# A graph network kernel: the order of weighing and digit reading, and of aggregating and turning the counts

## The chip, the cores and the metric

The kernel runs on one core of one Trainium2 chip. Its time is the device time of one execution in microseconds (us), given as the median of several runs.

## The reference

The input is a graph of 1250 nodes with 128 features each, and 20000 edges (src, dst) with four edge attributes. Two layers run one after the other, each with a residual.

```python
# layer 1: attention over the incoming edges, then one GRU step
h = relu(layernorm(x))
Wh = h @ W.T + b_W
e = leaky_relu((Wh @ a_src)[src] + (Wh @ a_dst)[dst] + a_b, 0.2)
attn = segment_softmax(e, dst)                # over the edges of one dst
h_prime = segment_sum(attn * Wh[src], dst) + h @ res_W.T + res_b
x = x + gru(h_prime, h)
# layer 2: four steps; an edge's type is the argmax of its attributes
h = relu(layernorm(x))
for _ in range(4):
    trans = einsum('nd,tod->tno', h, W_edge) + b_edge
    h = gru(segment_sum(trans[type, src], dst), h)
x = x + h
```

## The kernel before, in words

The nodes are padded to NT = 10 tiles of 128. The kernel never gathers edges in layer 1. It builds, for each block of 128 destination nodes (J or n, 0 to 9), a matrix of how many edges of each type run from each source to each destination, packed as digits, and computes attention densely on it.

A block has two windows of 64 destinations, numbered 2J and 2J+1. The edges are sorted by destination, and a window takes the edge tiles in which its destinations lie: 8 to 10 from J = 3 on (constant `TILES`). Per tile VectorE makes a one-hot row set (`one_hots`, line 967) in a ring of `RING = 12` slots, and TensorE multiplies it with a one-hot of the source lane and sums in PSUM (`window`, line 1468). VectorE may be at most 12 ahead (line 965). In some windows `one_hots` first makes a slice of lane one-hots (line 941, constant `LANES_MADE`; from J = 3 on for windows 7, 10 and 14).

The work on a block then passes over the engines:

- `evac(J, half)`, ScalarE, line 544: copies a window's sums from PSUM to SBUF. It waits for the window, and, as the target is used again, for `read_digits(J - 1)`.
- `read_digits(n)`, VectorE, lines 975 and 976: splits the words of block n into digits. It waits for both evacuations of the block.
- `count_turn(n)`, TensorE, line 1482: turns the digits into rows of counts in PSUM. It waits for the digits, and until the counts before have been copied out.
- `counts_out(n)` and `excesses(n)`, ScalarE, lines 556 and 562: copies the counts to SBUF and checks digits that ran over. It waits for `count_turn(n)` and for `weigh(n - 1)`, which reads the same buffer.
- `weigh(n)`, VectorE, line 986: ten instructions that multiply the counts with the attention weights. It waits for `counts_out(n)` (semaphore `K.counted`) and for `aggregate(n - 2)`.
- `aggregate(n)`, TensorE, line 1505: twenty matmuls with the weighed counts, whose last column is the denominator. It waits for `weigh(n)`.
- `reciprocals(n)`, VectorE, lines 1015 and 1019, waits for `aggregate(n)`; `attn_out(n)`, ScalarE, line 584, scales the result.

Each engine runs its list in the order written. On all three engines that order is by hand, in a function `turn(J)`. ScalarE's `turn(J)` (line 610) is: `evac(J - 1, 1)`, `attn_out(J - 3)`, `evac(J, 0)`, `counts_out(J - 1)`, `excesses(J - 1)`. VectorE's is at line 1021 and TensorE's at line 1520.

Behind the ten turns stands a tail. ScalarE has `evac(9, 1)`; VectorE has `read_digits(9)`, `weigh(8)`, `reciprocals(8)`, `weigh(9)`; TensorE has the residual matmuls, the first gates, `count_turn(9)`, `aggregate(8)`, and later `aggregate(9)` (lines 1666 to 1677). Then come layer 1's GRU and the four steps of layer 2, which don't use `turn`.

Of the kernel before, what the change touches and what calls it, by code (L numbers as in the profile page):

```python
# [93 lines left out]
def build(nc, x, src, dst, attr, W, b_W, a_src, a_dst, a_b, res_W, res_b, Wi, Wh_g, bi, bh,  # L94
          W_edge, b_edge, W_ih, W_hh, b_ih, b_hh, out):
    with ExitStack() as ctx:
# [212 lines left out]
        def there(n):  # L309
            return not isinstance(n, int) or 0 <= n < NT  # L310

        def later(n, k=1):
            return not isinstance(n, int) or n >= k


        def tile_ranges(eng, J):
            word = eng.value_load(table[0:1, J:J + 1], min_val=0, max_val=(1 << 26) - 1)
            first = eng.snap(word & 255)
            starts = [first]
            for shift in (8, 14, 20):  # L320
                starts.append(eng.snap(first + ((word >> shift) & AHEAD)))
            return (starts[0:2], starts[2:4])
# [42 lines left out]
        def weights(n):  # L365
            return exp_b if isinstance(n, int) and n % 2 else exp_a
# [484 lines left out]
        def _(dve):  # L851
# [58 lines left out]
            def edge_scales():  # L910
                dve.wait_ge(E1.bound, 1)
                up, down = edge_up[:].bitcast(I32), edge_down[:, 0:1].bitcast(I32)
                link(v.tensor_scalar(edge_up[:], edge_q[:, 3:4], ROOM, None, ALU.mult))
                link(v.tensor_scalar(up, up, 23, 23, ALU.logical_shift_right, ALU.logical_shift_left))
                v.tensor_scalar(down, up, -1.0, float(263 << 23), ALU.mult, ALU.add).then_inc(E1.scale, 1)
# [42 lines left out]
            def one_hots(j, starts):  # L958
                for k in range(LANES_MADE[j - 1] if j else 0, LANES_MADE[j]):
                    lane_hots(k)  # L960
                dve.wait_ge(K.cellw, j + 1)
                for b, before, tiles in window_hots(j, starts):
                    end = before + len(tiles)
                    if end > RING:
                        dve.wait_ge(K.slot, end - RING)
                    for q, tile in enumerate(tiles):
                        last = v.tensor_scalar(half_hot[:, (before + q) % RING], iota[:, b * HALF:(b + 1) * HALF],  # L967
                                               cell_w[:, j % CELL_SETS, bass.ds(tile, 1)],
                                               fields[:, 1, bass.ds(tile, 1)], ALU.is_equal, ALU.mult)
                    last.then_inc(K.pair, len(tiles))  # L970

            def read_digits(n):
                dve.wait_ge(K.evac, 2 * n + 2)
                pk = packed.rearrange("p (i d) -> p i d", i=NT)
                v.tensor_scalar(nibbles[:, 0, :, n * P:(n + 1) * P], pk, LOW_NIBBLES, None, ALU.bitwise_and)
                v.tensor_scalar(nibbles[:, 1, :, n * P:(n + 1) * P], pk, 4, LOW_NIBBLES,  # L976
                                ALU.logical_shift_right, ALU.bitwise_and).then_inc(K.digits, 1)

            def weigh(n):
                dve.wait_ge(K.counted, n + 1)  # L980
                if n == 0:
                    dve.wait_ge(S0.fallen, 1)
                if n >= 2:
                    dve.wait_ge(K.agg, n - 1)
                for i in range(NT):
                    last = v.scalar_tensor_tensor(weights(n)[:, i * P:(i + 1) * P], fall[:, n * P:(n + 1) * P],  # L986
                                                  s_tall[:, i:i + 1], count[:, i * P:(i + 1) * P], ALU.max, ALU.mult)
                last.then_inc(K.probs, 1)
# [24 lines left out]
            def reciprocals(n):  # L1013
                dve.wait_ge(K.agg, n + 1)
                v.tensor_scalar(denom[:], psD[:, P:P + 1], 1e-30, None, ALU.max).then_inc(K.denom, 1)
                dve.wait_ge(K.denom, n + 1)
                if later(n):
                    dve.wait_ge(K.attn, n)
                v.reciprocal(denom_r[:], denom[:]).then_inc(K.recip, 1)

            def turn(J):
                if there(J):
                    one_hots(2 * J, ranges[J][0])
                if J == 3:
                    reciprocals(0)
                if there(J - 1):
                    read_digits(J - 1)
                if J == 1:
                    peaks()
                    edge_scales()  # L1030
                if there(J - 2):
                    weigh(J - 2)
                if there(J):
                    one_hots(2 * J + 1, ranges[J][1])
                if there(J + 1):
                    ranges[J + 1] = tile_ranges(dve, J + 1)
                if J >= 3:
                    reciprocals(J - 2)

            def peaks():  # L1040
                dve.wait_ge(S0.s_rows, 1)
                v.tensor_reduce(s_peak[:], s_rows[:], AX.X, ALU.max).then_inc(S0.s_peak, 1)
                dve.wait_ge(S0.s_peak, 1)
                v.tensor_scalar(s_back[:], s_peak[:], dst_bias[:, 0:1], RISE, ALU.add, ALU.mult)
                link(v.tensor_scalar(s_up[:], s_src[:], s_peak[:, 0:1], SLOPE, ALU.subtract, ALU.mult))
                link(v.tensor_reduce(s_top[:], s_up[:], AX.X, ALU.min))
                v.tensor_scalar(s_up[:], s_up[:], -SLOPE * SPREAD, None, ALU.max).then_inc(S0.s_fall, 1)
# [3 lines left out]
            for J in range(NT):  # L1051
                turn(J)
# [328 lines left out]
        def _(pe):  # L1381
# [21 lines left out]
            def spans():  # L1403
                for lo in range(0, NP, 512):
                    yield lo, min(NP, lo + 512)
# [44 lines left out]
            def fall_rows():  # L1450
                pe.wait_ge(S0.s_rows, 1)
                for lo, hi in spans():
                    last = mm(smallf[:, lo:hi], b_cols[:], hT[:, lo:hi], start=True, stop=True)
                last.then_inc(S0.d_ps, 1)


            def window(j, half, starts, begin=0, until=NW * ETP):
                if later(j, 2):
                    pe.wait_ge(K.evac, j - 1)
                pe.wait_ge(S0.lanes, LANES_MADE[j])  # L1460
                for b, before, tiles in window_hots(j, starts):
                    if not begin <= before < until:
                        continue
                    end = before + len(tiles)
                    pe.wait_ge(K.pair, end)
                    for q, tile in enumerate(tiles):
                        u = before + q - HOTS_BEFORE[2 * j + b]
                        last = mm(big[:, 2 * half + b, 0:HALF],  # L1468
                                  lane_hot[:, :, bass.ds(tile, 1)].rearrange("p l a -> p (l a)"),
                                  half_hot[:, (before + q) % RING], start=(u == 0),  # L1470
                                  stop=(u == TILES[2 * j + b] - 1), skip_group_check=True)
                    last.then_inc(K.slot, len(tiles))
# [22 lines left out]
            def aggregate(n):  # L1495
                fast = isinstance(n, int)
                if fast:
                    pe.wait_ge(K.probs, n + 1)
                else:
                    pe.wait_ge(K.probsb, n + 1)  # L1500
                if later(n):
                    pe.wait_ge(K.attn, n)
                w = weights(n) if fast else probT
                for i in range(NT):
                    last = mm(psD[:, 0:P + 1], w[:, i * P:(i + 1) * P], Wh[:, i], start=(i == 0),  # L1505
                              stop=(i == NT - 1), skip_group_check=True)
                last.then_inc(K.agg, 1)
# [12 lines left out]
            def turn(J):  # L1520
                lower, upper = tile_ranges(pe, J)
                window(2 * J, 0, lower)
                if J == 1:
                    fall_rows()
                if J >= 2:
                    count_turn(J - 1)
                if J == 2:
                    edge_weights()
                if J >= 3:
                    aggregate(J - 2)  # L1530
                window(2 * J + 1, 1, upper)
                if J == 1:
                    count_turn(0)
# [12 lines left out]
            score_rows()  # L1546
            pe.wait_ge(C.ident16, 1)
            turn(1)
            turn(2)
            edge_biases()  # L1550
            pe.wait_ge(E1.rows, 1)
# [371 lines left out]
```

## Time and profile before

| | |
|---|---|
| median of 3 runs | 425.48 us (425.25 to 427.06) |
| profiled execution | 426.4 us, of it span 424.4 us |
| TensorE matmul busy | 367.2 us (87%) |
| VectorE busy | 265.5 us (63%) |
| ScalarE busy | 150.5 us (35%) |
| GpSimd busy | 100.6 us (24%) |
| mean granted TensorE clock | 0.974 |

The span is the time from the first to the last instruction of the profiled execution. Busy shares are means over stages with different limits. The attention stage with its turns lies between 23 and 158 us; from 178 us on the four steps of layer 2 run, in which TensorE is busy 232.34 of 246 us. The granted clock is TensorE's, as a share of the full 2.4 GHz; 0.50 is the level of 1.2 GHz.

### The profile page before, as it was taken

What the parts mean: (1) busy time and instruction counts of PE and PEld (TensorE: products, weight loads), DVE (VectorE), ACT (ScalarE), POOL (GpSimd) and SP (SyncE); (2) the same over time, 40 slices, a digit from 0 to 9 for tenths busy, and PEclk for the clock granted to TensorE, in tenths of its full rate; (3) what the DMA queues carried; (4) which work ended last, traced back from release to release, by engine and by line L of the source; (5) the groups of instructions that cost most, each with busy time, mean ns of one, the idle gap of its engine ahead of it and who ended that gap; (6) DMA issues with size and microseconds to landing.
All of it is one profiled execution on the core that took longest, in us unless ns stands there. A gap on an engine that the chain in (4) does not pass through costs nothing.

```text
span 424.4 us, 6625 instructions
## 1 busy us (share of the span) xinstructions
PE 367.2 (87%) x2057; PEld 247.0 (58%) x2057; DVE 265.5 (63%) x797; ACT 150.5 (35%) x333; POOL 100.6 (24%) x139
## 2 busy tenths in 40 slices
PE   1479758878798978888999999999999999999993
PEld 0457434656555866533557574756746575747792
DVE  6899958899989548686274544444443545434144
ACT  3354565444454535533122231322322232213021
POOL 3101100000000001010477400777003774007300
PEclk9999987999989989999999999999999999999997
DMA  5200000000000000112224201133202242012200
GB/s 146 73 1 2 0 2 1 2 1 2 2 1 2 0 2 0 49 51 102 73 53 151 81 34 74 45 105 100 87 2 93 58 148 87 26 74 52 56 14 23
DMA packets 14498, 19.88 MB, mean 47 GB/s; under 512 B 2591, under 2 KB 7728, under 8 KB 14460
## 3 DMA queue, kind: packets, MB, share of 16 engines
q1 hardware_dynamic: 10276, 12.90, 8.6%
q0 software_dynamic: 2912, 5.97, 5.7%
q10 hardware_dynamic: 1272, 0.54, 0.5%
q8 instruction: 19, 0.31, 0.3%
q14 instruction: 19, 0.16, 0.1%
HBM read 8.27 MB, written 11.13 MB: 46 GB/s over the span
## 4 chain that ended last, share of the span: by engine, by line
PE 69%; DVE 18%; issue 5%; ACT 4%; DVEq 2%; POOL 1%; DMA 0%; SPq 0%; ACTq 0%; POOLq 0%
PE small L1626 28%; PE big L1608 7%; PE small L1505 6%; PE big L1468 6%; DVE scores L986 3%; DVE cell_hot L967 3%; PE small L1482 3%; PE small L1647 2%; PE small L1660 2%; PE big L1571 1%; DVEq L967 1%; PE small L1571 1%; PE small L1562 1%; PE small L1573 1%; DVE digit_words L1137 1%
## 5 line engine op out<-in xcount | busy, mean ns | idle before, releaser
L1626 PE MATMUL small<-nibbles,store 128*128 128x384 fp8e4 (+1 forms) x640 | 125.8, 353 | 1.6 <-DVE store L1141 0.8
L482 POOL DMA_INDIRECT scores<-messages,w_gat x91 | 87.9, 966 | 120.5 <-DMA messages<-store 94.0
L1626 PEld LDWEIGHTS small<-nibbles,store 128*128 128x128 f16 x640 | 62.3, 98 | 64.6 <-issue 7.5
L967 DVE TENSOR_SCALAR cell_hot<-iota,cell_w,fields 128x320 bf16<-128x320 f16 x231 | 64.9, 358 | 0.9 <-issue 0.3
L1468 PE MATMUL big<-cell_hot,store 128*128 128x320 bf16 x231 | 44.8, 331 | 15.2 <-DVE cell_hot L967 12.9
L740 ACT CAST store<-digit_words 128x512 f16<-128x512 f32 x40 | 24.6, 618 | 81.6 <-DVE digit_words L1137 81.6
L1137 DVE TENSOR_TENSOR digit_words<-big,edge_rows 128x512 f32<-128x512 f32 x40 | 27.4, 690 | 40.0 <-PE big L1608 40.0
L1468 PEld LDWEIGHTS big<-cell_hot,store 128*128 x231 | 31.6, 145 | 26.1 <-issue 23.3
L1608 PE MATMUL big<-wT,h 128*128 128x512 f32 x80 | 38.6, 599 | 2.3 <-ACT h L736 2.3
L468 POOL TENSOR_TENSOR rstd<-var_e,power 128x2 f32<-128x2 f32 x5 | 3.5, 694 | 135.8 <-DVE var_e L1125 135.8
L1080 DVE SCALAR_TENSOR_TENSOR cell_hot<-rz,cell_hot 128x256 f32<-128x256 f32 (+2 forms) x29 | 11.0, 380 | 36.1 <-ACT cell_hot L711 36.1
L1482 PE MATMUL small<-nibbles,ident 128*128 128x512 fp8e4 (+1 forms) x120 | 26.4, 375 | 6.7 <-DVE nibbles L976 6.7
L1141 DVE TENSOR_TENSOR store<-digit_words,store 128x512 f16<-128x512 f32 x40 | 27.5, 689 | 6.1 <-ACT store L740 4.8
L710 ACT ACTIVATE rz<-small,gb 128x192 f32<-128x192 f32 (+1 forms) x14 | 6.2, 444 | 67.9 <-PE small L1573 67.9
L1505 PE MATMUL small<-Wh,scores 128*128 128x129 f32 x200 | 26.4, 290 | 2.7 <-DVE scores L986 1.7
L1505 PEld LDWEIGHTS small<-Wh,scores 128*128 128x128 f32 x200 | 24.8, 202 | 5.5 <-DVE scores L986 3.6
L986 DVE SCALAR_TENSOR_TENSOR scores<-scores,s_tall,tallies 128x128 f32<-128x128 f32 x100 | 27.1, 345 | 0.3 <-issue 0.3
L1482 PEld LDWEIGHTS small<-nibbles,ident 128*128 128x128 f16 x120 | 12.0, 105 | 20.8 <-DVE nibbles L976 8.6
L1253 DVE TENSOR_SCALAR aS<-small,edge_down 128x192 f32<-128x192 f32 (+2 forms) x24 | 9.7, 431 | 22.5 <-PE small L1626 17.6
L1608 PEld LDWEIGHTS big<-wT,h 128*128 128x128 f32 x80 | 14.5, 190 | 15.4 <-issue 10.6
L544 ACT CAST digit_words<-big 128x640 uint16<-128x640 f32 x20 | 13.8, 692 | 22.1 <-DVE nibbles L976 12.6
L556 ACT ACTIVATE tallies<-small 128x1280 f32<-128x1280 f32 x10 | 12.4, 1240 | 19.7 <-DVE scores L986 10.6
(262 smaller groups left out, 489.5 us busy)
## 6 DMA issues: line engine op xcount, KB each, us to landing
messages<-store SPq DMA_DIRECT2D x40, 256.0 KB, 2.0
scores<-messages,w_gat POOLq DMA_INDIRECT x91, 2.6
xn<-in_x SPq DMA_DIRECT2D x1, 576.0 KB
out<-xn SPq DMA_DIRECT2D x4, 128.0 KB
store<-in_edge_attr SPq DMA_DIRECT2D x1, 256.0 KB
wn<-in_L_gnn_W_edge SPq DMA_DIRECT2D x1, 256.0 KB, 6.3
wn<-in_L_gnn_Wi ACTq DMA_DIRECT2D x1, 192.0 KB, 3.8
wn<-in_L_gnn_Wh_g ACTq DMA_DIRECT2D x1, 192.0 KB, 6.0
```

The source lines that it names most:

```text
L482: g.indirect_dma_start(out=rows16[:, u].rearrange("p a f -> p (a f)"), out_offset=None, in_=table_rows[s % 2][:], in_offset=bass.IndirectO ...
L544: a.copy(o.rearrange("p i (b d) -> p b i d", b=2), big[:, 2 * half:2 * half + 2, 0:HALF].rearrange("p b (i d) -> p b i d", d=SUB)).then_in ...
L740: a.copy(m16[s % 2][:, i, :, 0], full[:, i % 2].rearrange("p (t o) -> p t o", t=TYPES)).then_inc(T.hi, 1)
L967: last = v.tensor_scalar(half_hot[:, (before + q) % RING], iota[:, b * HALF:(b + 1) * HALF], cell_w[:, j % CELL_SETS, bass.ds(tile, 1)], f ...
L986: last = v.scalar_tensor_tensor(weights(n)[:, i * P:(i + 1) * P], fall[:, n * P:(n + 1) * P], s_tall[:, i:i + 1], count[:, i * P:(i + 1) * ...
L1137: v.tensor_tensor(full[:, i % 2], big[:, i % 2], edge_rows[:], ALU.add).then_inc(T.full, 1)
L1141: v.tensor_tensor(m16[s % 2][:, i, :, 1], full[:, i % 2].rearrange("p (t o) -> p t o", t=TYPES), m16[s % 2][:, i, :, 0], ALU.subtract).the ...
L1468: last = mm(big[:, 2 * half + b, 0:HALF], lane_hot[:, :, bass.ds(tile, 1)].rearrange("p l a -> p (l a)"), half_hot[:, (before + q) % RING] ...
L1482: last = mm(smallf[:, lo:hi], ident16[:], A8[:, q // 2, lo // P:hi // P, n * P:(n + 1) * P, q % 2], start=(q == 0), stop=(q == TYPES - 1), ...
L1505: last = mm(psD[:, 0:P + 1], w[:, i * P:(i + 1) * P], Wh[:, i], start=(i == 0), stop=(i == NT - 1), skip_group_check=True)
L1608: mm(big[:, i % 2], h1[:, i * P:(i + 1) * P], wT[:, W_EDGE:NWT].rearrange("p t o -> p (t o)"), start=True, stop=True).then_inc(T.ps, 1)
L1626: last = mm(bank[:, 0:w], m16[s % 2][:, i, t, part], A8[:, t % 2, i, lo:lo + w, t // 2], start=(i == 0 and part == 0 and t == 0), stop=(i ...
```

## The change

Two calls change places in VectorE's turn, and two in TensorE's. VectorE now calls `weigh(J - 2)` before `read_digits(J - 1)`. TensorE now calls `aggregate(J - 2)` before `count_turn(J - 1)`. In J = 2 only VectorE's order changes, since TensorE's first aggregation has its own place ahead of J = 3. ScalarE's order and the tail are as they were.

```diff
@@ VectorE, turn(J)
                     one_hots(2 * J, ranges[J][0])
                 if J == 3:
                     reciprocals(0)
+                if there(J - 2):
+                    weigh(J - 2)
                 if there(J - 1):
                     read_digits(J - 1)
                 if J == 1:
                     peaks()
                     edge_scales()
-                if there(J - 2):
-                    weigh(J - 2)
                 if there(J):
                     one_hots(2 * J + 1, ranges[J][1])
@@ TensorE, turn(J)
                 window(2 * J, 0, lower)
                 if J == 1:
                     fall_rows()
+                if J >= 3:
+                    aggregate(J - 2)
                 if J >= 2:
                     count_turn(J - 1)
                 if J == 2:
                     edge_weights()
-                if J >= 3:
-                    aggregate(J - 2)
                 window(2 * J + 1, 1, upper)
```

## Rows read from the trace of the kernel before

**Rows 1.** The list of waits: engine, line waited for, total us, times, longest.

```profile
DVE denom L1015 <- PE small L1505: 13.7, 7, 5.5
```

**Rows 2.** Timeline of VectorE (start, us, line, operation, idle before): first digit passes.

```profile
75.72 0.47 DVE L975 TENSOR_SCALAR nibbles<-digit_words 128x1280 uint16<-128x1280 uint16 x1
...
86.49 0.49 DVE L975 TENSOR_SCALAR nibbles<-digit_words 128x1280 uint16<-128x1280 uint16 x1
...
96.77 0.48 DVE L975 TENSOR_SCALAR nibbles<-digit_words 128x1280 uint16<-128x1280 uint16 x1
...
115.64 0.49 DVE L975 TENSOR_SCALAR nibbles<-digit_words 128x1280 uint16<-128x1280 uint16 x1
...
125.36 0.48 DVE L975 TENSOR_SCALAR nibbles<-digit_words 128x1280 uint16<-128x1280 uint16 x1
...
134.15 0.48 DVE L975 TENSOR_SCALAR nibbles<-digit_words 128x1280 uint16<-128x1280 uint16 x1
...
141.72 0.49 DVE L975 TENSOR_SCALAR nibbles<-digit_words 128x1280 uint16<-128x1280 uint16 x1 [0.23 <-ACT digit_words L544]
```

**Rows 3.** Timeline of VectorE: turn J = 6, and the waits for aggregations.

```profile
103.36 2.41 DVE L967 TENSOR_SCALAR cell_hot<-iota,cell_w,fields 128x320 bf16<-128x320 f16 x8
105.69 0.48 DVE L975 TENSOR_SCALAR nibbles<-digit_words 128x1280 uint16<-128x1280 uint16 x1
...
106.49 2.71 DVE L986 SCALAR_TENSOR_TENSOR scores<-scores,s_tall,tallies 128x128 f32<-128x128 f32 x10
109.12 2.27 DVE L967 TENSOR_SCALAR cell_hot<-iota,cell_w,fields 128x320 bf16<-128x320 f16 x8
111.79 0.16 DVE L1015 TENSOR_SCALAR denom<-small 128x1 f32<-128x1 f32 x1 [0.41 <-PE small L1505]
...
122.55 0.16 DVE L1015 TENSOR_SCALAR denom<-small 128x1 f32<-128x1 f32 x1 [1.22 <-PE small L1505]
...
131.46 0.16 DVE L1015 TENSOR_SCALAR denom<-small 128x1 f32<-128x1 f32 x1 [0.41 <-PE small L1505]
```

**Rows 4.** Timeline of TensorE: aggregation, windows after gaps, last turn of the counts.

```profile
95.30 0.95 PE L1468 MATMUL big<-cell_hot,store 128*128 128x320 bf16 x5 [1.39 <-DVE cell_hot L967]
...
109.25 2.50 PE L1505 MATMUL small<-Wh,scores 128*128 128x129 f32 x20 [0.29 <-DVE scores L986]
111.59 1.25 PE L1468 MATMUL big<-cell_hot,store 128*128 128x320 bf16 x8
114.42 0.86 PE L1468 MATMUL big<-cell_hot,store 128*128 128x320 bf16 x4 [1.58 <-DVE cell_hot L967]
...
143.07 2.33 PE L1482 MATMUL small<-nibbles,ident 128*128 128x512 fp8e4 x12
...
152.08 0.70 PE L1562 MATMUL big<-hT,wT 128*128 128x256 f32 x2 [2.11 <-DVE cell_hot L1085]
```

**Rows 5.** Timeline of ScalarE: copying out of counts, and the last evacuation.

```profile
69.56 1.25 ACT L556 ACTIVATE tallies<-small 128x1280 f32<-128x1280 f32 x1
...
70.93 1.36 ACT L562 ACTIVATE tallies<-tallies,few 128x1280 bf16<-128x1280 f32 x1
...
140.93 0.69 ACT L544 CAST digit_words<-big 128x640 uint16<-128x640 f32 x1 [0.36 <-PE big L1468]
...
145.44 1.24 ACT L556 ACTIVATE tallies<-small 128x1280 f32<-128x1280 f32 x1 [3.16 <-PE small L1482]
```

**Rows 6.** Timeline of VectorE: the digits in J = 2.

```profile
63.55 0.49 DVE L975 TENSOR_SCALAR nibbles<-digit_words 128x1280 uint16<-128x1280 uint16 x1 [5.18 <-ACT digit_words L544]
```

**Rows 7.** Windows: stretch, length, busy (instructions) by engine, granted clock, DMA share, GB/s.

```profile
115.73:116.14 0.41, 0.41 (x3) 0.70 0.00 0
...
119.01:119.42 0.41, 0.41 (x2) 0.64 0.00 0
...
116.00:119.00 3.00, 3.00 (x10) 1.20 (x9) 3.00 (x12) 0.93 (x2) 0.00 (x0) 0.50 0.02 5
154.00:156.50 2.50, 2.50 (x13) 2.50 (x13) 0.00 (x0) 0.00 (x0) 0.00 (x0) 0.50 0.00 0
```

## The prediction

> **What bounds the kernel now.** I read the page first. TensorE is busy 87% of the span, but a mean over stages says little here, so I then read the list of waits. One of its rows [rows 1] belongs to the attention stage and to VectorE: it waits 13.7 us, in seven places, for an aggregation before it can read the denominator (line 1015). Last I read the timelines of VectorE, TensorE and ScalarE over the stage (64 to 158 us), which is where the price of a turn is. Between the start of one digit pass and the next lie 10.77, 10.28, 8.92, 9.95, 9.72 and 8.79 us, into J = 4 to 9 [rows 2, 3]. Inside a turn VectorE hardly stops: in J = 6 it makes 8 one-hots (103.36), reads the digits (105.69), weighs (106.49), makes 8 more (109.12) and then waits 0.41 us for the aggregation [rows 3]. Its waits before line 1015 are 0.41, 1.22 and 0.41 us at 111.79, 122.55 and 131.46. So VectorE's own work per turn is the bound (9.95 - 0.41 = 9.54 us in J = 7, where a slice of lane one-hots is made; 9.72 - 1.22 = 8.50 in J = 8; 8.79 - 0.41 = 8.38 in J = 9), and TensorE is close behind. Everything after the stage hangs on its end, since the GRU gates need the last two aggregations.
>
> **What moves.** No instruction is added or removed; two pairs change places in each turn J. I walk the queues with durations of the rows.
>
> (a) VectorE weighs block J-2 before it reads the digits of J-1. Weighing takes 2.63 us from start to next start (106.49 to 109.12), the two passes 0.80 (105.69 to 106.49) [rows 3]. For VectorE alone the sum is the same. weigh(J-2) starts 0.80 earlier and the digits 2.63 later. What hangs on the digits later is the half-0 evacuation by ScalarE and the turning of the counts on TensorE.
>
> (b) TensorE aggregates J-2 first (2.76 us after weighing begins, 106.49 to 109.25; it occupies 2.34, 109.25 to 111.59) and turns the counts of J-1 after it [rows 3, 4]. Before, the turn of the counts filled TensorE's time while VectorE weighed. Now that time is empty, and both come one behind the other after it, with window 2J+1 behind both. That window starts 2.76 + 2.34 + about 2.2 = 7.3 us after weighing starts. The 2.2 is count_turn(9), 143.07, less the last matmul's drain of about 0.2, taken from its 2.37 until ScalarE starts at 145.44 [rows 4, 5].
>
> (c) Two new loops follow. *Counts loop:* weigh(J-2), aggregate, turn the counts, copy them out, weigh(J-1). That is 2.76 + 2.34 + 2.37 (143.07 to 145.44) + 1.37 (69.56 to 70.93) = 8.84 us [rows 3 to 5]. *Ring loop:* VectorE may be 12 one-hots ahead of TensorE. Window 2J+1 has 8 tiles, so 4 of the next window fit; the others wait until TensorE has done the first pair of window 2J+1, at 7.3 + about 0.5 = 7.8 us. Four more at 0.28 (2.27 / 8 [rows 3]) make 8.9. In J = 6 (9 tiles, then 8) six are left: 7.8 + 1.7 = 9.5.
>
> (d) Turn by turn, from weigh(1), now at 75.72. J = 4: VectorE's 10.77 decides, 86.49. J = 5: 10.28, 96.77. J = 6: 9.5 against 8.92 before, 106.2. J = 7: lane slice, VectorE's 9.54, 115.8. J = 8: 8.9, 124.7. J = 9: 8.9, 133.6. The digit pass in that place stood at 134.15 [rows 2]: the turns themselves come out 0.5 us ahead, because 2.04 us of waits at line 1015 have gone (the longest of them behind a half-clock stretch), and 1.5 of waits in the two new loops have come.
>
> (e) The tail loses. ScalarE is in program order: counts_out(8) and excesses(8) stand ahead of evac(9, 1). After weigh(7) at 133.6: aggregate and turn 2.76 + 2.34 + 2.37, counts and excesses 2.73 (69.56 to 70.93, and 1.36), evacuation to digits 0.79 (140.93 to 141.72), digits 0.80 [rows 2, 3, 5]. That is 11.8 us, so weigh(8) starts at 145.4. Before, it started at 141.72 + 0.80 = 142.52. The 2.9 us come from ScalarE's copy, which stood beside window 19 and now stands behind the turn of the counts. What follows weigh(8) keeps its length. Bounds of this term: if VectorE's work alone set every turn (10.77, 10.28, 8.92, 9.54, 8.50, 8.38) weigh(7) would start at 132.1 and the loss is 1.4; with every ring and counts wait twice as long as I take them (1.5 more) it is 4.4. I take 2.9, since each loop is made of rows.
>
> (f) The first turns give nothing. In J = 2 VectorE waits 5.18 us for ScalarE before it reads the digits [rows 6], and weigh(0) now fits into that wait; VectorE comes free 2.63 us earlier. But reciprocals(0) still waits for aggregate(0), whose wait is on ScalarE's rows of biases. The count turn feeding that chain still waits for the same digits. Value 0; it could be 0 to 0.5.
>
> (g) TensorE's clock. The gap before a window or weighing was cut by the turn of the counts; now TensorE stands idle from the end of window 2J until 2.76 us after weighing starts, some 2.3 to 2.4 us, in each of seven turns. In the trace a gap of 1.58 us (to 114.42) is followed by granted clock 0.50 in 116 to 119, one of 2.11 us (to 152.08) by 0.50 in 154 to 156.5; a gap of 1.39 (to 95.30) is followed by none [rows 4, 7]. These are the 1.2 GHz and the 2.4 GHz level. The stretch from 115.9 to 119.3 lasts 3.4 us and costs 1.7 us of matmul. In J = 6, 8, 9 and the tail the path now runs through the aggregation and the turn of the counts, four places where a fall is paid in full; in J = 5 and 7 VectorE's lane slice covers most of it. Bounds: no fall (0) to a fall in all seven turns. I take three of the four paid, 3 x 1.7 = 5.1 us, the nearer to the rows, since two of the three gaps shown led to a fall, and the new gaps are longer than all three.
>
> The Trainium skill's page TensorE: Matmul & The Clock Gate, section "HAM oscillation", describes a loop in which the array waits in every iteration, is throttled again and begins each time at the lower clock. By it all turns would pay; the trace's 1.39 us gap without a fall speaks against so strict a reading, and the rival below prices it from rows. Whoever skips this paragraph loses no term.
>
> **Sum.** 2.9 + 0 + 5.1 = +8.0 us on the profiled execution's 426.4 us (span 424.4), that is 434.4. The median of the runs is 425.48, 0.9 lower, so I predict 433.5.
>
> **Rivals.**
> *Full clock.* The gaps trigger nothing, and only the two loops and the tail count: +2.9, 428.4 us. For it: the idle shares of the stage's turns do not grow, only the gaps join. Against it: both gaps above 1.5 us in the rows.
> *Cold in every turn.* Loop 8.84 + 1.7 = 10.5 in each turn from J = 5 (J = 4 keeps 10.77): weigh(7) at 86.49 + 5 x 10.5 = 139.0, tail 11.8 + 1.7, weigh(8) at 152.5 against 142.5: +10.0, 435.5 us.
> *VectorE is the only bound (the other side).* The waits at line 1015 go, the clock never falls because aggregation and turn form one long run, and the ring releases early enough. Weigh(7) starts at 132.1, +1.4 at weigh(8). If the half-clock stretch at 154 us, which sits on the aggregation of the last block, also goes away, -1.7: 425.2 us, not slower. It decides once window 2J+1 begins less than 7 us after weighing starts. For it: 2.04 us of waits at line 1015. Against: 2.76 + 2.34 + 2.2 are each rows of this trace, and ScalarE's order in the tail cannot be avoided.
>
> **How the numbers follow.** Forecast 0.55, own range 430.5 to 435. Full clock 0.2, cold in every turn 0.15, VectorE only 0.1. Range 428.0 to 436.5: it takes in full clock and cold in every turn. A measurement of this kernel tells about 0.5% (2.1 us) from no change; below 423.4 is faster, above 427.6 slower. The forecast, the cold case and most of full clock are slower: 0.87. Most of VectorE only and the low edge of full clock are same: 0.10. Faster 0.03.
>
> **What would show it.** Right if: the wait at line 1015 in J = 6 to 8 is gone; TensorE shows gaps of over 2 us ahead of line 1505 in each turn, released by VectorE's line 986; line 1482 starts at the end of 1505; ScalarE's line 556 waits for TensorE and no longer for line 986; the last evacuation starts some 10 us after weigh(7) starts; and more half-clock stretches stand between 75 and 150 us. The layers after 178 us must be the same length. Wrong if evac(9, 1) is not late against weigh(7), or if the granted clock of the stage is 1.00 throughout (then 428), or if VectorE waits for the counts by more than the loop of 8.84 says.

## The result, and the profile after

The changed kernel takes 436.34 us (median of 4 runs, 435.20 to 436.74), the kernel before 426.06 beside it: ratio 1.024, 95% interval 1.0223 to 1.0257. It is 10.3 us slower; the prediction was 433.5, with a range of 428.0 to 436.5. The profiled execution has a span of 434.5 us against 424.4.

First the list of waits of the changed kernel (engine, line waited for, total us, times, longest).

```profile
ACT tallies L556 <- PE small L1482: 35.0, 9, 4.9
...
DVE denom L1015 <- PE small L1505: 14.8, 6, 4.1
PE small L1505 <- DVE scores L986: 14.1, 7, 2.2
...
DVE cell_hot L967 <- PE big L1468: 6.3, 7, 2.4
```

ScalarE's copy of the counts (line 556) now waits for TensorE, 35.0 us in all, and TensorE's aggregation (1505) waits for the weighing in seven places. Two hops that ran beside each other now run one after the other. The row that answers to [rows 1] has hardly moved (13.7 to 14.8 us). Of the three waits that the prediction names, the two of 0.41 us went; the one of 1.22 us stayed as 1.17 (at 126.28), behind an aggregation on half clock. VectorE's wait for ring slots (967) is new.

VectorE's timeline of the changed kernel gives the turns; it answers to [rows 2, 3]. In these turns the weighing (986) is what the first digit pass was before.

```profile
77.98 2.69 DVE L986 SCALAR_TENSOR_TENSOR scores<-scores,s_tall,tallies 128x128 f32<-128x128 f32 x10
...
88.75 2.71 DVE L986 SCALAR_TENSOR_TENSOR scores<-scores,s_tall,tallies 128x128 f32<-128x128 f32 x10
...
100.10 2.70 DVE L986 SCALAR_TENSOR_TENSOR scores<-scores,s_tall,tallies 128x128 f32<-128x128 f32 x10
...
107.98 0.36 DVE L967 TENSOR_SCALAR cell_hot<-iota,cell_w,fields 128x320 bf16<-128x320 f16 x1 [0.88 <-PE big L1468]
...
109.95 2.71 DVE L986 SCALAR_TENSOR_TENSOR scores<-scores,s_tall,tallies 128x128 f32<-128x128 f32 x10
...
119.41 2.71 DVE L986 SCALAR_TENSOR_TENSOR scores<-scores,s_tall,tallies 128x128 f32<-128x128 f32 x10
...
130.46 2.71 DVE L986 SCALAR_TENSOR_TENSOR scores<-scores,s_tall,tallies 128x128 f32<-128x128 f32 x10
...
139.69 2.71 DVE L986 SCALAR_TENSOR_TENSOR scores<-scores,s_tall,tallies 128x128 f32<-128x128 f32 x10
...
152.29 0.49 DVE L975 TENSOR_SCALAR nibbles<-digit_words 128x1280 uint16<-128x1280 uint16 x1 [4.41 <-ACT digit_words L544]
...
153.10 2.71 DVE L986 SCALAR_TENSOR_TENSOR scores<-scores,s_tall,tallies 128x128 f32<-128x128 f32 x10
...
160.55 2.71 DVE L986 SCALAR_TENSOR_TENSOR scores<-scores,s_tall,tallies 128x128 f32<-128x128 f32 x10 [0.27 <-issue]
```

The starts lie 10.77, 11.35, 9.85, 9.46, 11.05 and 9.23 us apart for J = 4 to 9, against 10.77, 10.28, 8.92, 9.95, 9.72 and 8.79 before. From weigh(7) (139.69) to weigh(8) (153.10) it is 13.41 us, where the old order needed 8.38 (134.15 to 142.53).

TensorE of the changed kernel, answering to [rows 4]:

```profile
91.52 4.04 PE L1505 MATMUL small<-Wh,scores 128*128 128x129 f32 x20 [2.18 <-DVE scores L986]
...
122.17 4.07 PE L1505 MATMUL small<-Wh,scores 128*128 128x129 f32 x20 [2.04 <-DVE scores L986]
...
142.45 4.14 PE L1505 MATMUL small<-Wh,scores 128*128 128x129 f32 x20 [2.05 <-DVE scores L986]
146.43 2.33 PE L1482 MATMUL small<-nibbles,ident 128*128 128x512 fp8e4 x12
148.59 0.84 PE L1468 MATMUL big<-cell_hot,store 128*128 128x320 bf16 x5
...
165.57 2.40 PE L1505 MATMUL small<-Wh,scores 128*128 128x129 f32 x20
```

Ahead of each aggregation of the turns stands a gap of 1.70 to 2.18 us. The three shown (of blocks 2, 5 and 7) take over 4 us instead of 2.50; the other four take 2.50. The last row is aggregate(9), which had taken 4.01 us on the half clock before. ScalarE, answering to [rows 5], has the tail: the counts of block 8 (148.79), the check (150.15), and only then the last evacuation (151.51, before at 140.93).

```profile
148.79 1.24 ACT L556 ACTIVATE tallies<-small 128x1280 f32<-128x1280 f32 x1 [4.81 <-PE small L1482]
...
150.15 1.36 ACT L562 ACTIVATE tallies<-tallies,few 128x1280 bf16<-128x1280 f32 x1
...
151.51 0.67 ACT L544 CAST digit_words<-big 128x640 uint16<-128x640 f32 x1
```

The windows show the granted clock in the last columns (stretch, length, TensorE busy, clock, DMA share, GB/s). The last row is layer 2, where TensorE works 232 of 242 us at full clock.

```profile
91.00:95.00 4.00, 3.48 (x17) 0.57 0.00 0
...
122.00:126.00 4.00, 3.83 (x20) 0.57 0.00 0
...
142.00:146.00 4.00, 3.55 (x17) 0.57 0.00 0
...
152.00:156.00 4.00, 3.76 (x10) 0.60 0.00 0
178.00:420.00 242.00, 232.73 (x1280) 1.00 0.22 70
```

Between 76 and 160 us, four stretches have a mean clock of 0.57 to 0.60, where [rows 7] had two. Layer 2's matmuls of line 1626 start 10.4 us later than before (189.9 against 179.5), and the last matmul of the whole kernel 10.1 us later (430.96 against 420.86), so everything was lost ahead of layer 2.

The sum of the two profiled executions, by the starts of VectorE's rows:

| piece | before | after | difference |
|---|---|---|---|
| start of the first changed turn (digits(2), now weigh(1)) | 75.72 | 77.98 | +2.26 |
| turns J = 4 to 9 | 58.43 | 61.71 | +3.28 |
| to weigh(8) | 8.38 | 13.41 | +5.03 |
| weigh(8) to weigh(9) | 5.93 | 7.45 | +1.52 |
| weigh(9) to the matmul behind aggregate(9) | 8.89 | 7.25 | -1.64 |
| together | | | +10.45 |

Most of the first row isn't the change's. ScalarE's copy of block 0's counts starts 1.82 us later than before (58.77 against 56.95), and the first instruction that stands in another place, weigh(0), starts only at 60.13. Of these 1.82 us, 0.93 were there before TensorE's clock fell for the first time (the window at 38.95 before starts at 39.88); the rest came with a half-clock stretch that begins at 53.8 us instead of 51.0. The last 0.44 us came after 60 us, and for them the place of block 0 isn't excluded. Eight of the profiled executions are of kernels that are alike up to this point, but for the place of block 0. The stage starts at 75.72 in the two that have the old place, and at 76.21 to 77.98 in the six with block 0 early. It starts at 75.68 with block 0 early and 16 slots in the ring, so the early place alone doesn't make it late.

The last row is a fall that did not come. A gap of 2.11 us precedes the gates' matmuls in both kernels (152.08 before, 164.17 after); behind it the clock fell before and stayed at 1.00 after. No run shows that the order decides this.

### The profile page after: what moved, and what is told of

The parts are those of the page before. It is cut to its first block, busy times and chain, and to the rows that moved or that the text cites. A ratio compares the mean times of both kernels' runs of the same rounds, so it can differ in the third digit from the quotient of the medians.

```text
span 434.5 us, 6625 instructions
## 1 busy us (share of the span) xinstructions
PE 368.9 (85%) x2057; PEld 252.4 (58%) x2057; DVE 266.0 (61%) x797; ACT 149.6 (34%) x333; POOL 100.5 (23%) x139
## 4 chain that ended last, share of the span: by engine, by line
PE 69%; DVE 17%; issue 6%; ACT 5%; DVEq 2%; POOL 1%; DMA 0%; SPq 0%; ACTq 0%; POOLq 0%
PE small L1626 27%; PE big L1608 7%; PE small L1505 6%; PE small L1482 5%; PE big L1468 4%; DVE scores L986 3%; DVE cell_hot L967 3%; PE small L1647 2%; PE small L1660 2%; DVEq L967 1%; PE big L1571 1%; PE small L1571 1%; PE small L1562 1%; PE small L1573 1%; PE small L1572 1%
## 5 line engine op out<-in xcount | busy, mean ns | idle before, releaser
L1468 PE MATMUL big<-cell_hot,store 128*128 128x320 bf16 x231 | 41.6, 322 | 10.1 <-DVE cell_hot L967 8.6
L1505 PE MATMUL small<-Wh,scores 128*128 128x129 f32 x200 | 29.5, 312 | 15.4 <-DVE scores L986 14.1
L1505 PEld LDWEIGHTS small<-Wh,scores 128*128 128x128 f32 x200 | 27.9, 224 | 18.0 <-DVE scores L986 15.7
L544 ACT CAST digit_words<-big 128x640 uint16<-128x640 f32 x20 | 13.7, 684 | 18.6 <-DVE nibbles L976 18.6
```

What stands on the lines that cost most here:

```text
L544: a.copy(o.rearrange("p i (b d) -> p b i d", b=2), big[:, 2 * half:2 * half + 2, 0:HALF].rearrange("p b (i d) -> p b i d", d=SUB)).then_in ...
L1468: last = mm(big[:, 2 * half + b, 0:HALF], lane_hot[:, :, bass.ds(tile, 1)].rearrange("p l a -> p (l a)"), half_hot[:, (before + q) % RING] ...
```

## The experiments

All times are medians, with the kernel before run beside them on the same chip. The diffs are against the changed kernel, except where the text says otherwise.

**One half alone: VectorE's.** TensorE has the order of before.

```diff
-                if J >= 3:
-                    aggregate(J - 2)
                 if J >= 2:
                     count_turn(J - 1)
                 ...
+                if J >= 3:
+                    aggregate(J - 2)
```

> Only VectorE's order is changed (weigh before digits); TensorE turns the counts first, as before. My theory (two loops through TensorE): the counts are turned 3.6 us after weighing starts, the aggregation ends at 8.3, VectorE waits there 2.5 us in every turn at line 1015 and then still has to make the next window, so a turn takes about 11.1 us (12.3 with a lane slice): +10.8 us over J = 4 to 9, +2.2 in the tail, and gaps of 3.2 us on TensorE with falls of the clock: 439 to 443 us. Rival (VectorE's half is harmless, the loss is TensorE's order alone): 425 to 428 us.

453.49 us against 426.58, ratio 1.0625 (1.0592 to 1.0659). The mechanism was as told, and the size was too small by 10 us. TensorE's timeline, then a row of VectorE's:

```profile
92.50 4.45 PE L1482 MATMUL small<-nibbles,ident 128*128 128x512 fp8e4 x12 [2.99 <-DVE nibbles L976]
96.74 2.84 PE L1505 MATMUL small<-Wh,scores 128*128 128x129 f32 x20
```

```profile
99.61 0.16 DVE L1015 TENSOR_SCALAR denom<-small 128x1 f32<-128x1 f32 x1 [4.44 <-PE small L1505]
```

A gap of 2.99 us precedes the turn of the counts, which then takes 4.45 us instead of 2.34, and VectorE waits 4.44 us for the aggregation behind it. The expectation charged the clock once or twice, but from J = 4 on every turn of the counts pays (3.23 to 4.45 us, six times). The turns J = 4 to 9 take 79.43 us against 58.43 before, 21 more where 10.8 were expected.

**The other half alone: TensorE's.** VectorE reads the digits first.

```diff
-                if there(J - 2):
-                    weigh(J - 2)
                 if there(J - 1):
                     read_digits(J - 1)
                 ...
+                if there(J - 2):
+                    weigh(J - 2)
```

> Only TensorE's order is changed (aggregate before turning the counts); VectorE reads the digits first, as before. My theory: both loops are 0.8 us longer than with both halves changed (9.7 instead of 8.9 us), but VectorE's lane slices hide part: +2.0 us over J = 4 to 9, +4.2 in the tail, about +5 for the clock: 437 us (435 to 440). Rival (TensorE's half is the gain and VectorE's the loss): under 428 us. Rival (the two losses add up): 426 + part of 10.3, clearly under 436.

454.03 us, ratio 1.0662 (1.0631 to 1.0694), 17 us more than my theory gave. It had missed a third loop. ScalarE's and VectorE's timelines show it:

```profile
97.33 1.25 ACT L556 ACTIVATE tallies<-small 128x1280 f32<-128x1280 f32 x1 [8.01 <-PE small L1482]
...
98.69 1.36 ACT L562 ACTIVATE tallies<-tallies,few 128x1280 bf16<-128x1280 f32 x1
...
100.05 0.67 ACT L544 CAST digit_words<-big 128x640 uint16<-128x640 f32 x1
```

```profile
87.40 0.49 DVE L975 TENSOR_SCALAR nibbles<-digit_words 128x1280 uint16<-128x1280 uint16 x1 [0.62 <-ACT digit_words L544]
...
100.75 0.49 DVE L975 TENSOR_SCALAR nibbles<-digit_words 128x1280 uint16<-128x1280 uint16 x1 [1.00 <-ACT digit_words L544]
```

ScalarE copies the counts, checks them, and only then evacuates the upper window of the block whose digits VectorE reads next. With the digits first, VectorE stands before that evacuation in each turn (0.62 and 1.00 us). The loop is 0.80 + 2.76 + 2.34 + 2.37 + 2.73 + 0.79 = 11.8 us from digits to digits, and the first turn (75.72 to 87.40) measures 11.68; the later ones, with half clock in them, 13.4 to 14.0. In the full change the weighing stands ahead of the digits and hides this. So each half costs 27 us alone and both together 10: VectorE's half repairs most of what TensorE's does, and neither is a gain by itself.

**The old order in the last turn.** Both engines have the old order in J = 9 only.

```diff
-                if there(J - 2):
+                if there(J - 2) and J < NT - 1:
                     weigh(J - 2)
                 ...
+                if J == NT - 1:
+                    weigh(J - 2)
```

TensorE's `aggregate(J - 2)` goes back behind `count_turn(J - 1)` in J = 9 likewise (not shown).

> Both orders changed in J = 2 to 8, but J = 9 has the order of before on both engines, so that the last window's evacuation doesn't stand behind the turn of the counts. My theory (tail term 2.9 us, plus the half-clock stretch that fell on it, 1.5): 432 to 433.5 us. If the tail has no part in the loss: 436.

431.82 us, ratio 1.0141 (1.0106 to 1.0176), 4.5 us under the full change. VectorE:

```profile
128.44 2.71 DVE L986 SCALAR_TENSOR_TENSOR scores<-scores,s_tall,tallies 128x128 f32<-128x128 f32 x10
...
139.33 0.49 DVE L975 TENSOR_SCALAR nibbles<-digit_words 128x1280 uint16<-128x1280 uint16 x1 [1.58 <-ACT digit_words L544]
...
148.06 0.49 DVE L975 TENSOR_SCALAR nibbles<-digit_words 128x1280 uint16<-128x1280 uint16 x1 [0.23 <-ACT digit_words L544]
...
148.87 2.71 DVE L986 SCALAR_TENSOR_TENSOR scores<-scores,s_tall,tallies 128x128 f32<-128x128 f32 x10
```

From weigh(6) (128.44) to weigh(8) (148.87) it is 20.4 us; in the full change 22.6 (130.46 to 153.10). Changing back costs something too: VectorE waits 1.58 us before the digits of block 8, the evacuation loop of the run above. This kernel has three falls of the clock between 76 and 160 us and not four: on aggregate(2) and aggregate(5) as in the full change, and on the turn of the counts of block 8 (140.29, 4.02 us). The profiled execution is also the fastest of four (430.78), and its stage starts 1.77 us earlier. So the 4.5 us are the tail, part of the clock and perhaps some of the start, not the tail by itself.

**The clock held.** TensorE fills the gaps with matmuls that nobody reads.

```diff
+            def fill(n, counted):
+                pe.wait_ge(K.counted, counted)
+                for _ in range(n):
+                    mm(psA[:, 0:HALF], ident16[:], iota[:, 0:HALF], start=True, stop=True,
+                       skip_group_check=True)
 ...
                 if J >= 3:
+                    fill(14, J - 1)
                     aggregate(J - 2)
 ...
             residual(0, 2)
+            fill(14, NT - 1)
             pe.wait_ge(K.evac, NW)
```

> The changed kernel, with 14 matmuls of 320 columns, whose result nobody reads, on TensorE in the gap ahead of each aggregation of J = 3 to 9 and ahead of the wait for the last evacuation. My theory (four half-clock stretches of about 1.5 us each on the path): granted clock 1.00 from 76 to 160 us and 430 to 431 us. If the falls of the clock are covered by VectorE: 436, or a little more for the filling matmuls.

430.86 us, ratio 1.0096 (1.0079 to 1.0113). More work on TensorE, and the distance to the kernel before shrinks from 10.3 to 4.3 us. The window over the stage, and VectorE's rows:

```profile
76.00:160.00 84.00, 78.88 (x527) 0.99 0.01 1
```

```profile
76.80 2.69 DVE L986 SCALAR_TENSOR_TENSOR scores<-scores,s_tall,tallies 128x128 f32<-128x128 f32 x10
...
125.56 1.18 DVE L967 TENSOR_SCALAR cell_hot<-iota,cell_w,fields 128x320 bf16<-128x320 f16 x4 [1.11 <-PE big L1468]
...
135.89 2.71 DVE L986 SCALAR_TENSOR_TENSOR scores<-scores,s_tall,tallies 128x128 f32<-128x128 f32 x10
...
147.65 2.71 DVE L986 SCALAR_TENSOR_TENSOR scores<-scores,s_tall,tallies 128x128 f32<-128x128 f32 x10
...
153.57 2.71 DVE L986 SCALAR_TENSOR_TENSOR scores<-scores,s_tall,tallies 128x128 f32<-128x128 f32 x10 [0.27 <-issue]
```

Clock 0.99 where the changed kernel has 0.92, and what is left below 1 is the fall at 158 us that the kernel before had too. Weigh(1) to weigh(9) takes 76.77 us; the changed kernel has 82.57, before it was 72.74 (from digits(2) at 75.72 to 148.46). So the falls of the clock cost the changed kernel 5.8 us between weigh(1) and weigh(9), and without them it is 4.0 slower there than the kernel before. Of these 3.4 are the tail (135.89 to 147.65 is 11.76, before 8.38), and 0.66 the turns. But the kernel before has a fall of its own in J = 8, which counts against it in this comparison. Against the old order with the clock held (g1_before_fill below: 75.55 to 147.48, 71.93 us) the new order costs 4.8 us, 1.5 in the turns and 3.4 in the tail. The row at 125.56 is a wait for the ring.

**The ring.** The same with 16 slots; the four new ones lie in `rz`, which is free in this stage.

```diff
-RING = 12
+RING = 16
 ...
+        more_hot = rz[:].rearrange("p a b c -> p (a b c)").bitcast(BF16)[:, 0:4 * HALF].rearrange(
+            "p (u c) -> p u c", u=4)
```

> The changed kernel with the filling matmuls of e4_fill, and 16 slots for one-hots instead of 12 (the four new ones lie in a tile that is free in this stage). My theory (the ring of 12 makes J = 6, 8 and 9 longer than the counts loop of 8.84 us): VectorE's waits at line 967 for TensorE go, turns J = 6, 8 and 9 take 8.9, 8.9 and 8.9 us instead of 9.86, 9.49 and 9.23: about 2 us under e4_fill's ratio to the kernel before, 428.5 to 429.5 us. If the ring is not what lengthens them: 430.9 as e4_fill.

427.63 us, ratio 1.0034 (1.0015 to 1.0054), 0.6 points of the ratio (2.6 us) under e4_fill, where about 2 were expected; from weigh(1) to weigh(9) the traces differ by 2.07 us (74.70 against 76.77). VectorE no longer waits for slots in these turns:

```profile
96.72 2.72 DVE L993 SCALAR_TENSOR_TENSOR scores<-scores,s_tall,tallies 128x128 f32<-128x128 f32 x10
...
105.56 2.71 DVE L993 SCALAR_TENSOR_TENSOR scores<-scores,s_tall,tallies 128x128 f32<-128x128 f32 x10
...
115.03 2.71 DVE L993 SCALAR_TENSOR_TENSOR scores<-scores,s_tall,tallies 128x128 f32<-128x128 f32 x10
...
123.86 2.71 DVE L993 SCALAR_TENSOR_TENSOR scores<-scores,s_tall,tallies 128x128 f32<-128x128 f32 x10 [0.33 <-ACT tallies L563]
...
132.69 2.71 DVE L993 SCALAR_TENSOR_TENSOR scores<-scores,s_tall,tallies 128x128 f32<-128x128 f32 x10 [0.44 <-ACT tallies L563]
```

J = 6, 8 and 9 take 8.84, 8.83 and 8.83 us instead of 9.86, 9.49 and 9.23, and in the last two VectorE waits 0.33 and 0.44 us for ScalarE's copy of the counts. That is the counts loop, 8.84 us as worked out from the rows of before. So both loops exist; with 12 slots the ring is the longer one.

**Clock held and last turn old.** (Diff against e3_last_turn_old.)

```diff
-                if 3 <= J < NT - 1:
-                    aggregate(J - 2)
+                if 3 <= J < NT - 1:
+                    fill(14, J - 1)
+                    aggregate(J - 2)
```

> e3_last_turn_old with the filling matmuls of e4_fill in J = 3 to 8: both orders changed except in J = 9, clock held. My theory (the three terms add: clock 5.5, tail about 3, the rest ring waits): 427.5 to 428.5 us, still not under the kernel before. Rival (tail and clock are the same microseconds): 430 to 431 us.

427.26 us, ratio 1.0029 (1.0016 to 1.0042), just under what was expected: by the medians the terms add nearly as told. The traces give the order in J = 9 less. From weigh(6) to weigh(8) it is 19.29 us against 20.99 in e4_fill, 1.7 us less; another 1.3 us come from aggregate(9), which takes 2.40 us here and 3.71 on half clock there.

**The kernel before with the clock held.** The same filling at five places of the old order (diff against the kernel before).

```diff
             def turn(J):
+                if J == 2:
+                    fill(14, big[:, 0], K.evac, 3)
+                if J in (5, 7):
+                    fill(8, psA, K.counted, J - 1)
                 lower, upper = tile_ranges(pe, J)
                 window(2 * J, 0, lower)
 ...
+                if J == 2:
+                    fill(34, psA, K.counted, 1)
                 if J >= 2:
                     count_turn(J - 1)
 ...
             residual(1, 4)
+            fill(13, psA, K.counted, NT)
             cell_free(0)
```

> The kernel before, with filling matmuls in TensorE's gaps that were followed by half clock in its trace or were nearly as long (ahead of window 4, of count_turn(1), of the windows 10 and 14, and of the gates of chunk 1); their results are read by nobody. My theory (a gap on TensorE costs twice, by the half-clock stretch behind it, and these stretches lie on the path): granted clock 1.00 from 48 to 160 us and 420 to 422 us, under the kernel before by 4 to 6. Rival (half clock is mostly hidden by VectorE in the kernel before): 425 to 427 us.

423.81 us, ratio 0.9948 (0.9931 to 0.9965): faster, by half of what I expected. TensorE:

```profile
56.97 2.06 PE L1523 MATMUL big<-iota,ident 128*128 128x320 f16 x14
...
65.12 2.33 PE L1482 MATMUL small<-nibbles,ident 128*128 128x512 fp8e4 x12
...
68.32 1.24 PE L1468 MATMUL big<-cell_hot,store 128*128 128x320 bf16 x6 [0.44 <-DVE cell_hot L967]
```

The filling matmuls at 56.97 stand behind a gap and not in it: the gap is ahead of window 3, and I had put them ahead of window 4, so the fall at 52 to 55 us stayed. And where the turn of the counts became fast (65.12, 2.33 us instead of 4.10), window 5 waited for VectorE (0.44 us), which was weighing block 0. There the early weighing of J = 2 should be worth something.

**Block 0 early, by itself.** The kernel before with weigh(0) ahead of the digits in J = 2 (diff against the kernel before).

```diff
+                if J == 2:
+                    weigh(0)
                 if there(J - 1):
                     read_digits(J - 1)
                 ...
-                if there(J - 2):
+                if there(J - 2) and J > 2:
                     weigh(J - 2)
```

> The kernel before with one change: in J = 2 VectorE weighs block 0 before it reads the digits of block 1, so that weighing lies in a wait for ScalarE of 5.2 us. Both orders are as before in J = 3 to 9. My theory (the chain in J = 2 goes through ScalarE and not through VectorE): no change, 426 to 427 us. Rival (the stage begins earlier, as VectorE comes free 2.6 us sooner): 424 us or less. Rival (the early part of the change is what delays the stage's start by 2.3 us in the profile of after): 428 to 429 us.

426.03 us, ratio 0.9997 (0.9984 to 1.0010): no change in time, as step (f) said. Whether block 0's place moves the start of the stage is another question, which this doesn't settle. In the profiled execution the digits of block 2 are read at 77.74, 2.0 us later than before, and the span is 424.8 us all the same, since the last aggregation takes 2.40 us instead of 4.01.

**Both together.** (Diff against g1_before_fill.)

```diff
-        fill(34, psA, K.counted, 1)
+        fill(31, psA, K.counted, 1)
 ...
+                if J == 2:
+                    weigh(0)
```

> g1_before_fill with 31 instead of 34 filling matmuls ahead of count_turn(1), and block 0 weighed ahead of the digits in J = 2 alone. In g1's trace TensorE waited for window 5's one-hots behind the now fast count_turn(1) (0.44 us at 68.32) and the filling matmuls ran 0.4 us too long. My theory (with the clock held, VectorE's weighing is what comes last in J = 2): the stage begins about 1.4 us earlier, 422.0 to 422.8 us. If g4's result (block 0's place does not matter) holds also with the clock held: 423.5 to 424.

422.23 us, ratio 0.9907 (0.9893 to 0.9921). This is the fastest version, 14 us under the changed kernel and under the one before by 0.9%. The first aggregation starts at 71.72 (72.91 in the kernel before, 72.73 in g1_before_fill):

```profile
71.72 2.50 PE L1507 MATMUL small<-Wh,scores 128*128 128x129 f32 x20 [1.38 <-ACT edge_rows L693]
```

What gave nothing at the old clock gives 1.0 us at the start of the stage once the clock no longer covers it, and 1.6 us by the medians. The smaller number of filling matmuls is not what gave it: the turn of the counts behind them starts at 65.09 us, and at 65.12 in g1_before_fill.

**The new order with all mended.** The change in J = 2 to 8, the old order in J = 9, 16 slots, and the filling matmuls of h1 and e4. (Only the filling is shown.)

```diff
+                if J == 2:
+                    fill(14, 3, big[:, 0], K.evac)
 ...
+                if 3 <= J < NT - 1:
+                    fill(14, J - 1)
 ...
+                if J == 2:
+                    fill(31, 1)
 ...
+            fill(13, NT)
             cell_free(0)
```

> The changed order in J = 2 to 8 with everything that the runs so far found against it mended: clock held by filling matmuls (also those of h1), a ring of 16, and the order of before in J = 9. My theory: per turn the old order costs the same as the new at best, as VectorE's own work of 8.4 to 10.8 us bounds both and the counts loop is 8.84: 423.5 to 424.5 us, 1 to 2 us above h1. Rival (the new order was good and only its side effects bad): under h1, 421 us or less.

423.82 us, ratio 0.9951 (0.9932 to 0.9969), 1.6 us above h1 and as expected. The profiled execution, at 425.96, is 2.1 us over this median. VectorE:

```profile
74.74 2.69 DVE L993 SCALAR_TENSOR_TENSOR scores<-scores,s_tall,tallies 128x128 f32<-128x128 f32 x10
...
122.92 2.72 DVE L993 SCALAR_TENSOR_TENSOR scores<-scores,s_tall,tallies 128x128 f32<-128x128 f32 x10 [0.33 <-ACT tallies L563]
...
133.83 0.49 DVE L982 TENSOR_SCALAR nibbles<-digit_words 128x1280 uint16<-128x1280 uint16 x1 [2.51 <-ACT digit_words L551]
```

From weigh(1) to weigh(6) the new order takes 48.18 us; the old one, in h1, takes 48.84 over the same turns (74.53 to 123.37). So with a larger ring and a full clock the new order gains 0.66 us in five turns. It loses 3.9 going back to the old order (weigh(6) to weigh(8) takes 20.32 us, in h1 16.38): the digits wait 2.51 us for ScalarE, and a half-clock stretch falls on 134 to 138 us as well, where J = 9 has no filling. Whether a better tail would bring it under h1 wasn't tried.

## Why the prediction was right

The direction, the loops, the tail and the wide range hold; the sum of 8.0 us came out at 10.3. Point by point:

- (b) *TensorE runs aggregation and turn of the counts one behind the other, after a gap.* Right: gaps of 1.70 to 2.18 us ahead of line 1505 in the turns, against 2.3 to 2.4 forecast (the forecast was too long, and its "over 2 us in each turn" holds for five of the seven), and line 1482 starts where 1505 ends.
- (c) *Counts loop 8.84 us.* Right, by g2: 8.84 us once and 8.83 twice. In the changed kernel itself it never showed, as the ring loop is longer.
- (c) *Ring loop 8.9 us, and 9.5 in J = 6.* Right in kind, too short in size: 9.86, 9.49 and 9.23 with the clock held. The term "7.3 + about 0.5 us until the first slot is free" was mis-sized. In J = 9 of e4 VectorE goes on 8.1 us after weighing starts (126.66 to 134.79) instead of 7.8, and in J = 8 after 8.4 (117.17 to 125.56). That is 1.3 us over three turns, nearly all that the full-clock part was off (2.9 forecast; 4.0 in the stage, 4.3 by the medians).
- (d) *The turns come out 0.5 us ahead of before.* Wrong by just this: +0.66 with the clock held, +3.28 with the falls. The half microsecond was in any case not the order's. It came from VectorE's wait of 1.22 us in J = 8, and with the clock held in the old order (g1) that turn takes 8.90 us instead of 9.72; against that kernel the new order loses 1.5 us in the turns. In the changed kernel that wait did not go (1.17 us), so this sign of being right was missing; it goes with the clock held.
- (e) *The tail, 11.8 us to weigh(8).* Right: 11.76 in e4. The changed kernel has 13.41, the rest being a half-clock stretch on aggregate(7). Its price against the old order is 3.4 us, of which the forecast's 2.9 is what remained after the half microsecond of (d). "What follows weigh(8) keeps its length" did not hold: weigh(8) to weigh(9) took 7.45 us instead of 5.93, and the piece behind it 7.25 instead of 8.89, both by the clock.
- (f) *Block 0 early gives nothing.* Right (g4), with a condition that I had not seen: only while the turn of the counts runs at half clock.
- (g) *Three falls on the path, 5.1 us.* Right in kind: the clock was 5.8 us in the stage. That the size came so near is partly luck. The reason given, that the new gaps are longer than the three in the rows, did not hold: six of the seven are shorter than 2.11 us. Of the places forecast (J = 6, 8, 9 and the tail) J = 8 had a fall and the tail had two, on aggregate(7) and on the last turn of the counts; J = 6 and 9 had none. The fourth fell ahead of weigh(3), in J = 5, which was said to be mostly covered by VectorE's lane slice; that turn took 11.35 us instead of 10.28, so 1.07 of 1.7 us was paid.
- *The sum.* The 10.45 us between the profiled executions are 4.03 for the order (2.9 forecast), 5.80 for the clock (5.1), and 0.62 for what lies outside weigh(1) to weigh(9): +2.26 ahead and -1.64 behind, which the forecast put at nothing and no run ties to the change. With 436.34 us the kernel lies outside the forecast's own range of 430.5 to 435, and 0.16 us inside the wide one. That one was drawn to hold "cold in every turn", whose mechanism the runs exclude, so that it held is luck in part.
- *Rivals.* "Full clock" is excluded by the windows, and e4 shows what it would have given (430.9, not the 428.4 worked out). "Cold in every turn" is excluded as well: three of the seven gaps ahead of an aggregation led to a fall, the others did not. Its number (435.5) was nearer to the measured one than the forecast's all the same. "VectorE is the only bound" is excluded by the row at 125.56 and by g2.

What stays open: which of two gaps of equal length a fall follows. The changed kernel has a gap of 2.05 us ahead of 112.72 without one and one of 2.04 ahead of 122.17 with one. The gap of 2.11 us ahead of the second gates was followed by a fall in the kernel before and in e4_fill, and by none in the changed kernel, e3, g3 and g4 (2.12 us there). Even gaps of 2.50 and 2.51 us in J = 3 of the two halves had none. No run here varied a gap by itself.

## What to carry to other kernels

Before swapping two steps on an engine, walk the loop that the swap closes through all engines; here two hops that ran beside each other became one chain of 8.84 us, and the step of another engine that stands in program order behind it (ScalarE's last evacuation) moved by more than the turns themselves. Half of a swap can be far worse than the whole, so try both halves, but judge neither from the other's result. Where TensorE waits about 2 us in every turn, price the half-clock stretch behind the gap and not only the gap: filling it with matmuls that nobody reads made both orders faster, by 6.0 us and by 2.4.

## What the runs showed of the hardware that I had not expected

The half-clock stretches behind gaps of about 2 us cost nearly as much again as the gaps: 1.53 to 1.65 us where they lay fully on the path (changed kernel against e4_fill), 1.07 in J = 5. And they are not tied to the code alone: the stretch near 52 us begins at 51.0 in the kernel before and at 53.8 in the changed one, though the instructions until then are the same. The Trainium skill's page TensorE: Matmul & The Clock Gate, section "HAM oscillation", told of a loop that starts cold in every iteration. The full change paid in some turns only, while VectorE's half alone, with gaps of 2.77 to 2.99 us, paid in each of the six from J = 4 on (3.23 to 4.45 us for a turn of the counts that takes 2.34).
